# Inverse norms of queries and keys as a power of -1/2 on GpSimd, in the local blocks of a two-layer kernel

## The reference

```
qkv = shift_tokens(x) @ Wqkv               # 16 heads of 64
q = q / max(norm(q), 1e-12) * q_scale      # l2norm, per token and head
k = k / max(norm(k), 1e-12) * k_scale
q, k = rotary with a scale (xpos)
out = local attention, window 32, sim * 8, softmax
x = out @ Wo + x
x = (a * gelu(gate)) @ W2 + b2 + x         # from layernorm(shift_tokens(x)) @ W1 + b1
```

## Time and profile before

| what | value |
|---|---|
| median of 3 runs | 3686.81 us (3684.1 to 3694.66) |
| the profiled execution's own time | 3684.8 us |
| its span, first to last instruction | 3683.0 us |
| mean granted TensorE clock | 0.962 of 2.4 GHz |
| PE / DVE / ACT / POOL busy, share of the span | 89% / 74% / 55% / 30% |
| stretch of the local blocks | about 1241 to 3232 us from the span's start |

### The profile page before, as it was taken

How to read it: one execution, slowest core, us unless ns; L and a number is a source line. 1 busy time by engine, 2 the same in 40 slices (tenths; PEclk the granted TensorE clock), 3 DMA queues, 4 the chain that set the end, 5 groups by cost and what they waited for, 6 DMA issues and landing times. The chain is left out here.

```text
span 3683.0 us, 71336 instructions
## 1 busy us (share of the span) xinstructions
PE 3280.8 (89%) x25164; PEld 1821.2 (49%) x25164; DVE 2741.0 (74%) x3715; ACT 2013.3 (55%) x2780; POOL 1119.2 (30%) x709
## 2 busy tenths in 40 slices
PE   4999999999995688888888888888889888869997
PEld 2222222222224455556555565656555565548886
DVE  2777777777753598979888797989898887946664
ACT  2455555555551366666667676766666676621111
POOL 2000000000001464645455454555464454610000
PEclk7899999999995799999999999999999999979999
DMA  3000000000002210011011001001110110100001
GB/s 114 11 16 15 14 15 15 15 15 15 15 14 93 66 29 24 29 48 34 18 35 48 24 29 54 29 24 29 53 29 23 29 35 21 32 23 1 0 0 29
DMA packets 70710, 107.05 MB, mean 29 GB/s; under 512 B 26790, under 2 KB 41012, under 8 KB 69684
## 3 DMA queue, kind: packets, MB, share of 16 engines
q1 hardware_dynamic: 69716, 104.37, 9.8%
q10 hardware_dynamic: 864, 0.79, 0.1%
HBM read 38.79 MB, written 15.73 MB: 15 GB/s over the span
## 5 line engine op out<-in xcount | busy, mean ns | idle before, releaser
L924 DVE TENSOR_REDUCE a_part_max<-a_ps_max 128x1 f32<-128x512 f32 x1024 | 683.2, 691 | 290.6 <-PE a_ps_max L846 288.7
L822 ACT ACTIVATE a_expT<-a_ps_scoresT 128x1024 f32<-128x1024 f32 x512 | 517.0, 1024 | 314.6 <-PE a_ps_scoresT L858 309.2
L1614 DVE STREAM_TRANSPOSE b_probsT<-b_probs 32x1024 f32<-32x1024 f32 x384 | 474.3, 1235 | 94.3 <-POOL b_probs L1240 85.2
L867 PE MATMUL a_ps_out<-a_expT,a_v_op 128*32 128x512 f32 x2048 | 537.6, 605 | 0.7 <-issue 0.5
L1216 POOL TENSOR_TENSOR b_turned_q<-b_rot_q,b_turned_q 128x1024 f32<-128x1024 f32 x96 | 226.8, 2363 | 711.3 <-DVE b_turned_q L1548 711.3
L846 PE MATMUL a_ps_max<-a_k_op,a_q_op 96*128 96x512 bf16 x1024 | 401.3, 392 | 25.7 <-DMA a_k_op<-terms_k 21.8
L846 PEld LDWEIGHTS a_ps_max<-a_k_op,a_q_op 96*128 96x128 bf16 x1024 | 98.3, 96 | 516.2 <-DVE a_part_max L924 428.6
L1441 PE MATMUL b_psD<-b_probsT,b_v 128*64 128x128 f32 x3072 | 337.8, 278 | 5.8 <-DVE b_probsT L1614 5.8
L1442 PE MATMUL b_psD<-b_probsT,b_v_back 128*64 128x128 f32 x3072 | 332.8, 274 | 0.0
L1456 PE MATMUL b_psD<-b_w_qkv,b_xs 128*128 (+1 forms) x384 | 211.3, 638 | 111.6 <-ACT b_outT L1305 111.6
L858 PE MATMUL a_ps_scoresT<-a_q_op,a_k_op 128*128 128x512 bf16 x1024 | 306.8, 380 | 0.0
(11 more groups left out here) (294 smaller groups left out, 5907.9 us busy)
## 6 DMA issues: line engine op xcount, KB each, us to landing
b_v_back<-b_v SPq DMA_DIRECT2D x96, 384.0 KB, 3.5
b_v_back<-b_v SPq DMA_DIRECT2D x96, 128.0 KB, 3.4
b_w_qkv<-L_ffn_Wqkv SPq DMA_DIRECT2D x6, 1536.0 KB
sums<-a_outT SPq DMA_DIRECT2D x512, 16.0 KB
j_got<-sums SPq DMA_DIRECT2D x16, 512.0 KB
a_q_op<-terms_q SPq DMA_DIRECT2D x64, 48.0 KB
a_k_op<-terms_k SPq DMA_DIRECT2D x64, 48.0 KB
b_w_o<-L_ffn_Wo SPq DMA_DIRECT2D x6, 512.0 KB
```

What stands on the lines that cost most here:

```text
L822: act.activation(expT[kt % RING][:], ps_scoresT[kt % 2][:], ACT.Exp, scale=SCALE_A).then_inc(exp_ready, 1)
L867: last_mm = pe.matmul(ps_out[lo:lo + 32, :], v_op[(u // 2) % 2][:, kt, :], expT[kt % RING][:, 512 * half:512 * half + 512], start=(kt < 2) ...
L924: dve.tensor_reduce(part_max[:, qt, half:half + 1], ps_max[half][:], AX.X, ALU.max).then_inc(max_taken, 1)
L1614: dve.transpose(probsT[rows, :, :, rows].rearrange("p c h q -> p h c q"), probs[rows]).then_inc(probsT_ready, 1)
```

## The change

The root on ACT and the Exp that preloads the table go; the reciprocal on DVE goes. DVE now raises the squared norm itself to a floor of 1e-24, at the place where it raised the norm, and POOL takes `floored ** -0.5` with a `tensor_tensor` whose second operand is a tile of -0.5, between the copy of the next tokens and the multiplication of the queries. A `memset` of that tile is added at the start.

```diff
-        unused = sb("unused", [P, 1])
-        norm = sb("norm", [P, 2 * HEADS_B])
+        minus_half = sb("minus_half", [P, 2 * HEADS_B])
...
+            pool.memset(minus_half[:], -0.5).then_inc(zeroed, 1)
-            pool.wait_ge(zeroed, 4)
+            pool.wait_ge(zeroed, 5)
...
                     tokens_of((b * T8 + s + 1) % TILES, 1 - par)
+                    pool.wait_ge(unit_k_ready, T)
+                    pool.wait_ge(floored_ready, T + 1)
+                    pool.tensor_tensor(inv_norm[:], floored[:], minus_half[:], ALU.pow).then_inc(inv_norm_ready, 1)
                     unit(rot_q, turned_q, sum_q_ready, unit_q_ready, qT_half, 0)
...
                     act.activation(square_k[:], psK[:], ACT.Square).then_inc(square_k_ready, 1)
-                    act.wait_ge(norm2_ready, 2 * T + 2)
-                    act.wait_ge(floored_ready, T)
-                    act.activation(norm[:], norm2[:], ACT.Sqrt).then_inc(norm_ready, 1)
...
-                if 1 in lags:
-                    act.activation(unused[:], res["eps"][:, 0:1], ACT.Exp)
...
-                    dve.wait_ge(norm_ready, T)
+                    dve.wait_ge(floored_ready, T)
                     squared_norm(square_q, square_q_ready, 0)
...
-                    dve.wait_ge(norm_ready, T + 1)
-                    dve.tensor_scalar(floored[:], norm[:], NORM_FLOOR, None, ALU.max).then_inc(floored_ready, 1)
-                    dve.wait_ge(floored_ready, T + 1)
-                    dve.wait_ge(unit_k_ready, T)
-                    dve.reciprocal(inv_norm[:], floored[:]).then_inc(inv_norm_ready, 1)
+                    dve.wait_ge(norm2_ready, 2 * T + 2)
+                    dve.wait_ge(inv_norm_ready, T)
+                    dve.tensor_scalar(floored[:], norm2[:], NORM2_FLOOR, None, ALU.max).then_inc(floored_ready, 1)
```

More of the change, by code:

```diff
@@ L31 @@
 QK_SCALE = 8.0
-NORM_FLOOR = 1e-12
+NORM2_FLOOR = 1e-24
 GROUP = 512
@@ L1029, in local_blocks @@
         norm2_ready = sem("norm2_ready")
-        norm_ready = sem("norm_ready")
         floored_ready = sem("floored_ready")
@@ L1189, in _ @@
             pool.memset(probsT[:], 0.0).then_inc(zeroed, 1)
-            pool.wait_ge(zeroed, 4)
+            pool.memset(minus_half[:], -0.5).then_inc(zeroed, 1)
+            pool.wait_ge(zeroed, 5)
             for b in range(BATCHES):
                 pool.memset(y[64:P, column(b * T8):column(b * T8) + 1], 0.0).then_inc(zeroed, 1)
-            pool.wait_ge(zeroed, 6)
+            pool.wait_ge(zeroed, 7)
             def tokens_of(t, par):
```

## The result

The changed kernel takes 4011.62 us (median of 4 runs, 4010.79 to 4013.12) against 3685.45 us of the kernel before (4 runs): a ratio of 1.0882, 95% interval 1.086 to 1.0904, or 326 us more. The prediction said 3651 us, range 3643 to 3764. What came is its first rival, beyond the point where the range ended: the power does not fit.

A forecast was written before the change was run, and what follows sets the result against it. DVE's list with one POOL instruction in it was taken to bound each step. 95 steps x 0.38 us took 36.1 us off 3684.8, giving 3648.7; with 2.0 for the median, 3651 us, range 3643 to 3764.

The forecast's parts named there:

- first rival: Power on POOL above 1.98 us delays the probabilities; at 2.79 us the kernel takes 3764 us; chance 0.31.
- What bounds the kernel: In the local blocks, a step is DVE's own list plus POOL's L1240 of 1.90 us ahead of DVE's transposes.
- DVE, 0.38 us a step, 36 us: Without the reciprocal and the late wait for the floor, DVE's subtraction starts 0.38 us sooner; 95 steps gain 36 us.
- The floor is held by POOL's add: DVE's floor ends at 1967.13, held by POOL's add ending at 1967.09; its end was left unchanged.
- ACT, nothing: ACT loses two table loads, root and preloading Exp, 2.99 us a step, off the path; counted as no gain.
- POOL's budget of 1.60 us, break-even at 1.98: On POOL, a power up to 1.60 us is hidden ahead of the probabilities; at 1.98 us the gain is used up.
- X: Length of the new power instruction on POOL, taken as 1.0 us.
- The length of the power, 1.0 us: Power of 32 columns on POOL taken as 1.0 us, some 12 times an add's price per column.
- The upper bound: Power's length on POOL bounded from above by POOL's longest two-input instruction, 2.79 us.

The follow-up runs named there:

- the run with DVE's part alone: Kernel before, with the reciprocal dropped and the floor writing the tile POOL reads; root and table loads stay on ACT: 3650.62 us, ratio 0.9907.
- the split version: Changed kernel with power and floor in two halves of 16 columns, the queries' ahead of their add, the keys' behind the probabilities: 3889.59 us.
- the run with ACT's part alone: Kernel before, with the root made a copy and the preloading Exp dropped; DVE's floor and reciprocal stay: 3680.18 us, ratio 0.9993.
- the table: Changed kernel with a multiplication for the power, or the power over 8, 12, 16 or 32 columns: 3651.6, 3652.0, 3700.4, 3765.3, 4011.6 us.

## Why the prediction was wrong, by its own steps

*What bounds the kernel.* Right. A step is DVE's list with POOL's L1240 in it, and each kernel above whose power in one piece was too long paid in just that wait.

*DVE, 0.38 us a step, 36 us.* Right in size: the subtraction starts 0.37 us sooner in the trace, and the run with DVE's part alone gained 33 us. The step is only 0.33 us shorter (31 us in 95 steps), since the subtraction itself now takes 1.22 us instead of 1.16; why it does, no run shows. The reason given, an overlap that comes back once the wait for the floor goes, was half of it. The subtraction's own wait for the row maximum sets where it starts, and the floor lies under that.

*The floor is held by POOL's add.* Borne out by accident in the split version, with a later POOL instruction in the add's place. There the rule of the Trainium skill ("SBUF — State Buffer", "SBUF: two separate sides") is seen at work: the floor ends 0.03 us after POOL's instruction. The kernel before shows it too: in 80 of the 96 steps the floor ends 0.03 to 0.05 us after POOL's add, and in the 15 in which POOL is idle beside it, it takes 0.17 us. The prediction counted nothing for DVE being held up by the power itself. Beside the 5.44 us the keys' cosine part and the row sum take 1.21 and 1.22 us, as they do in the kernel before.

*ACT, nothing.* Right, shown by the run with ACT's part alone (0.9993). The reason told was half of it: the first copy comes sooner, but PE then waits as long for the second one, which follows DVE, so that its wait was 116.5 us in that run and 93.9 in the changed kernel, against 111.6 before.

*POOL's budget of 1.60 us, break-even at 1.98.* Right to 0.1 us: 1.65 us is free and gives the full gain, the growth of the periods puts the budget at 1.70, and 2.28 us is 0.46% slower than before. With X = 5.44 the prediction's own formula gives 3650.7 + 95 x (5.44 - 1.60) = 4015 us against 4011.6.

*The length of the power, 1.0 us.* This is the step that failed: 5.44 us. The power costs (5.44 - 1.65) / 24 = 0.158 us a column, 73 times the add's 2.15 ns, where the prediction had put 12 times. The upper bound was the fault behind it. POOL's longest two-input instruction of 2.79 us bounds nothing about an operator that no row shows; it is only a large number from the same list. The rival that came true was named with the right mechanism and price per us; what was wrong is the size of this one term. So the range ended in the middle of a case to which the text itself gave a chance of 0.31, and that chance rested on 26 times an add's price looking like much, for which no row spoke either.

## What to carry to other kernels

Work out the budget first: how long may the new instruction be before something behind it in its queue is late, and what does each us beyond that cost, times the steps. Here both came from a dozen rows, and with the measured X the prediction's formula gives each time of the table to 0.4%. Where the operation is not in the trace, its duration is then the whole bet, and it is better measured in one small run, or the range opened past the break-even, than bounded by its neighbours in the list. And an engine with much idle time is no free place for work: POOL was 30% busy, but only 1.7 us of its idle time a step lay between the place of the new instruction and the one that DVE waits for.

## What the runs showed of the hardware that was not expected

- A power on POOL takes 0.38 us + 0.158 us a column over 128 partitions (1.65, 2.28, 2.91 and 5.44 us at 8, 12, 16 and 32 columns), a multiplication of 32 columns 0.25 us.
- A DVE floor of 0.31 us between a reduction and the instruction that waits for the reduction's result cost nothing: 1.36 us from start to start with and without it.
- A DVE floor of 16 columns that takes 0.17 us took 0.91 beside a POOL multiplication and ended 0.03 us after it.
- Logarithm and exponential in a row cost a table load each, 192 in the stretch, where one set for both was hoped for.
- PE's granted clock in the stretch was 0.95 of the 2.4 GHz level after the change, 0.93 with the power in two halves and 0.99 before. It had done the same work with more idle time between. In the periods that are alike it adds nothing: they grow by X - 1.70 at 12 columns, with 0.99, as at 32, with 0.95. What it adds elsewhere was not measured by itself.
